# Fixed places for layer 0's maxima units, and bank uses straight behind the values product in 21 of 36 steps

## The reference, cut to what matters

```python
qkv = x @ Wqkv
q = qkv[..., :2 * Hx].reshape(Bx, 2 * NQ, Sx, HD)        # 32 heads of 16
k = qkv[..., 2 * Hx:2 * Hx + G].reshape(Bx, NKV, Sx, HD) # 8 heads, each for 4 query heads
v = qkv[..., 2 * Hx + G:].reshape(Bx, NKV, Sx, HD)
scores = jnp.einsum('bhqd,bhkd->bhqk', q, k) / math.sqrt(HD)
scores = jnp.where(causal, scores, -jnp.inf)
aw = jax.nn.softmax(scores, axis=-1)
aw = aw[:, :, 0] - lam * aw[:, :, 1]
attn = jnp.einsum('bhqk,bhkd->bhqd', aw, v) * (1.0 - LAMBDA_INIT)
```

## Time and profile before

| | us |
|---|---|
| median of 3 runs | 2282.1 |
| lowest, highest | 2281.39, 2282.92 |
| the profiled execution's own time | 2283.89 |
| its span, first to last instruction | 2282.1 |

### The profile page before, as it was taken

How to read it: one execution, slowest core, us unless ns; L and a number is a source line. 1 busy time by engine, 2 the same in 40 slices (tenths; PEclk the granted TensorE clock), 3 DMA queues, 4 the chain that set the end, 5 groups by cost and what they waited for, 6 DMA issues and landing times. The chain is left out here.

```text
span 2282.1 us, 45663 instructions
## 1 busy us (share of the span) xinstructions
PE 2114.3 (93%) x16684; PEld 927.0 (41%) x16684; DVE 1758.6 (77%) x4030; ACT 1551.3 (68%) x3249; POOL 654.6 (29%) x1219
## 2 busy tenths in 40 slices
PE   6799999999999999999999999999999698989983
PEld 5143333333333333333333333333332287567731
DVE  3888888888888888888888888888885277244477
ACT  2078787877878787878787787878787445146633
POOL 2214142332313232414233231313211044000077
PEclk8599999999999999999999999999999799999955
DMA  5230312222121303031222212130200300000001
GB/s 150 41 63 11 67 25 52 38 39 50 27 50 32 65 12 71 10 67 24 54 38 40 50 27 50 32 64 8 45 2 2 103 0 0 1 1 2 1 28 46
DMA packets 129528, 84.74 MB, mean 37 GB/s; under 512 B 90273, under 2 KB 119073, under 8 KB 129313
## 3 DMA queue, kind: packets, MB, share of 16 engines
q1 hardware_dynamic: 129312, 81.91, 18.2%
HBM read 26.81 MB, written 16.78 MB: 19 GB/s over the span
## 5 line engine op out<-in xcount | busy, mean ns | idle before, releaser
L755 ACT ACTIVATE probs<-b_bank 128x512 f32<-128x512 f32 (+1 forms) x2304 | 1171.8, 578 | 347.2 <-PE b_bank L915 336.1
L632 DVE TENSOR_REDUCE m_part<-a_bank 128x1 f32<-128x512 f32 (+3 forms) x2048 | 1190.5, 634 | 153.1 <-PE a_bank L885 111.0
L915 PE MATMUL b_bank<-q_pack,k_pack 34*128 34x512 bf16 (+7 forms) x5120 | 920.8, 348 | 4.4 <-DMA q_pack<-m_rows 2.9
L885 PE MATMUL a_bank<-k_pack,q_pack 64*128 64x512 bf16 (+3 forms) x2560 | 811.1, 357 | 54.3 <-DVE m_part L632 30.7
L957 PE MATMUL acc<-probs,v_tile 128*32 128x512 f32 (+3 forms) x5120 | 586.7, 539 | 3.1 <-POOL probs L498 0.8
L915 PEld LDWEIGHTS b_bank<-q_pack,k_pack 34*128 34x128 bf16 (+1 forms) x5120 | 310.6, 94 | 511.9 <-ACT probs L755 436.3
L885 PEld LDWEIGHTS a_bank<-k_pack,q_pack 64*128 64x128 bf16 x2560 | 226.0, 94 | 343.7 <-DVE m_part L632 209.7
L498 POOL TENSOR_SCALAR_AFFINE_SELECT probs<-probs 128x512 f32<-128x512 f32 (+1 forms) x192 | 151.7, 790 | 609.7 <-ACT probs L755 609.6
L629 DVE CUSTOM_DVE_ANT_0 a_bank<-a_bank,mask_a 128x128 f32<-128x128 f32 (+3 forms) x512 | 241.8, 512 | 66.7 <-PE a_bank L885 66.7
L957 PEld LDWEIGHTS acc<-probs,v_tile 128*32 128x32 f32 x5120 | 107.8, 108 | 174.8 <-issue 117.8
L895 PE MATMUL a_bank<-future,pick 64*128 64x128 bf16 x1024 | 134.4, 219 | 0.0
(11 more groups left out here) (199 smaller groups left out, 1869.9 us busy)
## 6 DMA issues: line engine op xcount, KB each, us to landing
q_pack<-part SPq DMA_DIRECT2D x384, 64.0 KB, 2.3
k_pack<-part SPq DMA_DIRECT2D x192, 64.0 KB, 2.3
headT<-scratch SPq DMA_DIRECT2D x80, 128.0 KB, 4.0
scratch<-qkvT SPq DMA_DIRECT2D x16, 512.0 KB, 2.8
xg<-in_L_attn_x SPq DMA_DIRECT2D x16, 256.0 KB, 2.8
scratch<-qkvT SPq DMA_DIRECT2D x32, 128.0 KB, 2.7
q_pack<-m_rows SPq DMA_DIRECT2D x256, 2.0 KB
x<-in_L_attn_x SPq DMA_DIRECT2D x4, 1024.0 KB, 11.6
```

The source lines that it names most:

```text
L632: dve.tensor_reduce(out, bank[:, 0:w], AX.X, ALU.max).then_inc(a_maxed, 1)
L755: act.activation(probs[:, n % P_RING, h, at:C], b_bank[bank_no(("B", n, h))][:, at:C], ACT.Exp, scale=HD ** -0.5) \
L885: ins = pe.matmul(a_bank[at % A_RING][:, 0:w], q_pack[buf][rows, hp, 0, q:q + P], k_pack[buf][rows, 0, C * c:C * c + w], start=True, stop= ...
L915: ins = pe.matmul(b_bank[bank_no(slot)][:, at:at + C - q], k_pack[par][rows, n2, P * kt:P * (kt + 1)], q_pack[par][rows, h // 2, n2, C * j ...
```

## The change

Five edits, all in layer 0's attention.

- `masked` becomes a fixed set of 12 units instead of the 16 diagonal units of the first pair of heads.
- `schedule()` and its table of times go. `PLACES` gives, for each of the 36 steps, how many units stand in each of five places: woven into heads 0 and 1 (first), behind them and before the values product (between), woven into heads 2 and 3 (second), behind those (behind), and last in the step (last). The sum is still 80 units a group.
- The transposes and projections of a step ("N", "W", "M", "O") stand directly behind the values product, before heads 2 and 3, in the 21 steps of `EARLY`; in the others they stay behind heads 2 and 3. ScalarE takes them in the same order, and the ring of score banks is numbered to match (`SLOTS`).
- "N" moves from step 4 to step 6, the six "W" from steps 6 to 11 to steps 8 to 13.
- VectorE's loop keeps its code; the number of units in a step follows `ENDS`, which now comes from `PLACES`.

```diff
+MASKED = {0, 1, 11, 15, 18, 40, 41, 55, 63, 71, 78, 79}
 def masked(u):
-    j, _, c, hp = A_UNITS[u]
-    return c == j and hp == 0
+    return u in MASKED

-PREP_AT = {4: ("N", 0), **{6 + w: ("W", w) for w in range(WPARTS)}}
+PREP_AT = {6: ("N", 0), 8: ("W", 0), 9: ("W", 1), 10: ("W", 2), 11: ("W", 3), 12: ("W", 4), 13: ("W", 5)}
-ENDS = schedule()
+EARLY = {0, 1, 3, 4, 5, 7, 12, 13, 16, 18, 19, 20, 22, 23, 25, 27, 28, 29, 32, 33, 35}
+PLACES = [[int(units) for units in step] for step in (
+    "11000 01000 01000 10000 11000 11002 11000 11100 11010 11000 11111 11001 "
+    "11000 11000 11000 11100 11000 11000 01000 11001 11000 01110 11000 01100 "
+    "11000 10000 11100 11000 11000 11000 11000 11000 11000 11000 11100 11000").split()]
+ENDS = [sum(map(sum, PLACES[:s + 1])) for s in range(STEPS)]
+def places(n):
+    left = list(units(n)) if n < LAST_STEP else []
+    out = []
+    for count in PLACES[n % STEPS]:
+        out.append(left[:count])
+        left = left[count:]
+    return out

-SLOTS = [slot for n in range(TAIL) for slot in [("B", n, h) for h in range(QH) if n < LAST_STEP] + uses_at(n)]
+SLOTS = [slot for n in range(TAIL) for half in range(2)
+         for slot in [("B", n, 2 * half + h) for h in range(2) if n < LAST_STEP] + uses_at(n) * ((n % STEPS in EARLY) != half)]
...
 # ScalarE
                 for h in range(QH):
                     if n < LAST_STEP:
                         exponential(n, h)
                     if h == 1 and n in COPY_AT:
                         take_output(COPY_AT[n])
+                    if h == 1 and s in EARLY:
+                        take_uses(n)
+                if s not in EARLY:
+                    take_uses(n)
...
 # TensorE
-                if n < LAST_STEP:
-                    two_heads(n, 0, ahead[0] if ahead else None)
+                first, between, second, behind, last = places(n)
+                if n < LAST_STEP:
+                    two_heads(n, 0, first[0] if first else None)
+                for u in between:
+                    score_maxima(u)
                 if LAG <= n < LAST_STEP + LAG:
                     meet_v(n - LAG)
-                if n < LAST_STEP:
-                    two_heads(n, 1, ahead[1] if len(ahead) > 1 else None)
-                for use in uses_at(n):
-                    ...
-                for u in ahead[2:]:
+                if s in EARLY:
+                    turn_and_project(n)
+                if n < LAST_STEP:
+                    two_heads(n, 1, second[0] if second else None)
+                for u in behind:
+                    score_maxima(u)
+                if s not in EARLY:
+                    turn_and_project(n)
+                for u in last:
                     score_maxima(u)
```

More of the change, by code:

```diff
@@ L87 @@
 GATES_AT = 24
[L88 to L109, removed]
-ENDS = schedule()
+EARLY = {0, 1, 3, 4, 5, 7, 12, 13, 16, 18, 19, 20, 22, 23, 25, 27, 28, 29, 32, 33, 35}
[4 more added lines that the diff above has]
+ENDS = [sum(map(sum, PLACES[:s + 1])) for s in range(STEPS)]
 A_LAST = [max(u for u in range(UNITS) if A_UNITS[u][0] == j) for j in range(NJ)]
+LAST_STEP = STEPS * GROUPS
 def units_by(n):
@@ L124, in units @@
     return range(units_by(n - 1), units_by(n))
-LAST_STEP = STEPS * GROUPS
+def places(n):
[5 more added lines that the diff above has]
+    return out
 NEXT = [j for j in range(NJ) if A_LAST[j] < LEAD]
@@ L768, in take_rows_of_output, with take_uses @@
                 act.activation(o_rows[:, :], bank[:, :], ACT.Copy).then_inc(o_taken, 1)
-            for n in range(TAIL):
-                g, s = n // STEPS, n % STEPS
-                for h in range(QH):
-                    if n < LAST_STEP:
-                        exponential(n, h)
-                    if h == 1 and n in COPY_AT:
-                        take_output(COPY_AT[n])
+            def take_uses(n):
                 for use in uses_at(n):
@@ L786, in _ @@
                         take_rows_of_output(k, no, bank)
+            for n in range(TAIL):
+                g, s = n // STEPS, n % STEPS
+                for h in range(QH):
+                    if n < LAST_STEP:
+                        exponential(n, h)
+                    if h == 1 and n in COPY_AT:
+                        take_output(COPY_AT[n])
+                    if h == 1 and s in EARLY:
+                        take_uses(n)
+                if s not in EARLY:
+                    take_uses(n)
                 if g + 2 < GROUPS and s in FIRST_AT:
@@ L969, in _, with turn_and_project @@
                     turn_maxima(m)
[L971 to L978, removed]
-                if n < LAST_STEP:
-                    two_heads(n, 0, ahead[0] if ahead else None)
-                if LAG <= n < LAST_STEP + LAG:
-                    meet_v(n - LAG)
-                if n < LAST_STEP:
-                    two_heads(n, 1, ahead[1] if len(ahead) > 1 else None)
+            def turn_and_project(n):
                 for use in uses_at(n):
@@ L995, in _ @@
                         turn_output(k, bank)
-                for u in ahead[2:]:
+            pe.wait_ge(m_copied, len(NEXT))
+            for n in range(TAIL):
+                g, s = n // STEPS, n % STEPS
+                ahead = list(units(n)) if n < LAST_STEP else []
+                if n < LAST_STEP and s in J_FIRST:
+                    pe.wait_ge(m_rows_in, 16 * QH * (NJ * g + J_FIRST.index(s) + 1))
+                if any(u % UNITS == 0 for u in ahead):
+                    pe.wait_ge(packs_in, 16 * PACK_DMAS * (ahead[-1] // UNITS + 1))
+                first, between, second, behind, last = places(n)
[3 more added lines that the diff above has]
+                    score_maxima(u)
+                if LAG <= n < LAST_STEP + LAG:
+                    meet_v(n - LAG)
+                if s in EARLY:
+                    turn_and_project(n)
+                if n < LAST_STEP:
+                    two_heads(n, 1, second[0] if second else None)
[4 more added lines that the diff above has]
+                for u in last:
                     score_maxima(u)
```

## The result

| | before | after |
|---|---|---|
| median us | 2282.5 (4 runs) | 2458.0 (4 runs, 2456.9 to 2461.9) |
| ratio | 1 | 1.0766, 95% interval 1.0752 to 1.078 |
| span of the profiled execution, us | 2282.1 | 2455.2 |
| one group, product to product, mean us | 106.0 | 117.3 |

The change costs 175 us. The forecast was 2417: the side and the mechanism hold, the size was 41 us short. The measured time lies outside the forecast's own range (2370 to 2450) and 2 us inside the wide one (2320 to 2460).

What follows compares the result with a forecast made beforehand. TensorE's issue order was taken as the bound: 96.0 - 0.4 - 1.0 + 20 of waits = 114.6 us a group against 106.0; over 15.6 groups +134, lead +1, 2282 + 135 = 2417 us. Own range 2370 to 2450, wide 2320 to 2460.

Steps and rivals of the forecast that it cites:

- The deciding term: Second unit's fourth head, before the values product: VectorE frees its bank at 1.18 us, issue wants 0.66, wait 0.52.
- even places win: Rival: the fourth head's wait vanishes and old bunches go; 98.6 us a group, 2167 us; chance 0.08.
- 12 with two units: Gaps between products with a full unmasked first unit and no third: 0.52 us wait each, 6.2 a group.
- 2 with a first unit VectorE masks: Gaps between products where VectorE's masked reduction takes 0.73 us: 0.62 of wait each, 1.2 a group.
- 5 with a narrow or masked first unit: Gaps between products with a narrow or TensorE-masked first unit: 0.2 to 0.4 us wait each, 1.6 a group.
- 10 with three units or more: Gaps between products bound by VectorE, 3.65 us against 2.63 of issue: 1.0 each, 10.5 a group.
- step 2's unit behind `normalise`: Step 2's unit waits 0.5 us for VectorE, which has two masked units, a block maximum and `normalise` first.
- The early uses: Uses directly behind the values product: 7 of 15 a group save a turn, 0 to 1.4 us together, taken as 1.0.
- The rival on ScalarE: In-order ScalarE holds exponentials of heads 2 and 3 behind a use: 7 uses, up to 0.5 us each, 2470; chance 0.04.
- The masks: Four fewer masked units save TensorE 0.44 us a group; VectorE gets 8 more masked reductions, 1.0 us.
- M and O come at least a step after what they read: Early "M" and "O" uses behind the values product were priced at 0 waiting cost.
- The rule on overtaking: TensorE matmuls keep program order, so the 0.52 us counts in full; overtaking by 0.1 would take off 45 us.

Runs made afterwards that it cites:

- experiment 1: The changed kernel with every unit that stood between woven into heads 2 and 3 instead, or put behind; 2347.2 us, ratio 1.0279 to the kernel before.
- experiment 2: The kernel before with each step's second unit issued by itself between heads 0 and 1 and the values product; 2509.5 us, ratio 1.0992.
- 7: The changed kernel with between units woven into heads 2 and 3, and block 2's maxima rows issued ahead of the next group's pack; 2295.6 us, ratio 1.0057.
- 10: The changed kernel with only block 2's maxima rows issued ahead of the next group's pack on SyncE; 2449.5 us, ratio 1.0734 to the kernel before.
- experiment 6: The changed kernel with VectorE's plain reductions over only the first half of a unit's columns; 2338.7 us, ratio 1.0249 to the kernel before.
- 9: The changed kernel with plain reductions halved and block 2's maxima rows issued ahead of the pack; 2279.8 us, ratio 0.9986 to the kernel before.
- experiment 5: The changed kernel with early uses undone, all transposes and projections behind heads 2 and 3 again; 2467.7 us, ratio 1.0809 to the kernel before.
- experiment 3: The kernel before with the early uses alone, in the same 21 steps; 2306.2 us, ratio 1.0099.
- experiment 4: The kernel before with the new set of masked units alone, units per step held at the old list; 2277.2 us, ratio 0.9972.

## Why the prediction was right, and where it was short

**The deciding term held.** The fourth head starts 1.17 us after the first, as forecast from the earlier trace rows, and product to product is 2.93 against a forecast 2.96. Experiments 1 and 2, and the pair 7 and 10, move only the place and move the time both ways; experiment 6, and the pair 9 and 10, move only the length of the reduction and take out 0.27 of that gap. The rival "even places win" was decided by the point it named, and lost.

**The size.** Gap by gap, what is left of each when the issue is taken off at the prediction's prices comes to waits of 22.4 us a group; I had 20. (The same account gives the kernel before 10.7, where I had 10.) These are estimates, since the prices are. The terms as I had set them:

| gaps of a group | forecast | measured |
|---|---|---|
| 12 with two units | 6.2 | 6.8 |
| 2 with a first unit VectorE masks | 1.2 | 1.0 |
| 5 with a narrow or masked first unit | 1.6 | 1.8 |
| 10 with three units or more | 10.5 | 12.3 |
| step 2's unit behind `normalise` | 0.5 | 0.6, and 0.6 in the kernel before too |

The mis-sized term is the ten crowded gaps, which I priced as if all held three units. Those behind steps 5, 10, 11 and 21 hold four or more units, or a unit issued by itself directly ahead of two more: they wait 1.5 to 1.8 each where I had about 1.0. The text let narrow units make up for them, and they do not. Among the twelve, the gap behind step 8 in truth holds a third unit, with a projection between, and waits some 0.8; the one behind step 9 includes some 0.4 for the maxima rows. The step 2 unit was no new wait: its gap is 2.09 us, 2.10 before. The issue itself comes to 94.9 us by this account, where I had 94.6. The two differences, 2.4 and 0.3, are 2.7 us a group, and times 15.6 they are 42 us, where 41 were missing.

**The range** held by luck. It was to cover waits of 14 to 24 us, but by the prediction's own sum 24 gives 118.6 us a group and 2480 us in all, not 2460. The measured time lies 2 us inside the edge; waits of 23 would by the same sum have been outside a range that was meant to hold them.

**The early uses** I put at 1.0 us a group and they gave 0.84 (experiment 5), though I counted seven where there are eight, and one of them costs time: part of the agreement is luck. The bounds 0 to 1.4 were too narrow below: in the kernel before the same edit costs 1.6 (experiment 3). On the four-bank ring a place behind a product can put ScalarE in the way (shown for "N"), and a use may also be cover for VectorE (argued from the steps that lost). The rival on ScalarE had the right engine for "N" in the old step 4, by another path; in the changed list "N" stands in step 6, which is not in `EARLY`.

**The masks** gave 0.34 a group against 0.44 (experiment 4); VectorE's extra work cost at most some tenths.

**SyncE's queue.** I checked the heads' DMAs and not the maxima rows, which stand behind the pack in the same queue. "M and O come at least a step after what they read" looked at the engines and missed what follows an "M". In the changed kernel this costs 8 us in all (experiment 10), hidden by the larger waits; with these gone it is the next bound (experiments 1 and 6).

**The rule on overtaking.** No row of the changed kernel shows the product passing the waiting head: it starts 0.31 behind it (800.40, 800.71). So the 0.52 counts in full. The Trainium skill, "TensorE: Matmul & The Clock Gate", Part 3 (The mechanism), says that matmuls keep their order, and for these two the trace agrees.

**Account of the 175 us.** Between places 154 (experiments 7 and 10); the rows' wait 8 (10); early uses -10 (5); masks -6 (4, measured in the old kernel). The rest, some 29, falls to the new counts per step and the later projections. It is a difference; neither was run by itself.

## What to carry to other kernels

With a ring of n banks between two engines, work out for every pair of neighbours in the issue order how far apart the ring lets them be, and compare it with how far apart the order puts them: moving one item from "woven into" to "right behind" can cost a full wait in every step, while VectorE looks 78% busy (92.0 of 117.3 us here) and TensorE's record says 93% (109.5). Spread such items so that the slow consumer's time passes under work that needs nothing from it, and count gaps with three and four items apart from those with two. A gain in one step is worth only what the next step's engines, and the DMA queue behind them, let through: after each quickened stretch look for the transfer that is now late.

## What the runs showed of the hardware

A stall can cost TensorE twice. In experiment 1 an idle stretch of 2.64 us, at a granted clock of 1.00, was followed by one at 0.71 and one at 0.50, with the same projection at 2.07 us in place of 1.13. It did not follow every time: the clock fell in 10 of the 14 groups that had such a wait. Nor does it take one long stall. Waits of 0.5 us in nearly every step left the clock at 1.00 through the changed kernel's groups until a wait of 1.62 us for the rows near their end (at 1791.6 us, clock at 0.50 from 1799.0). But in experiment 2, whose gaps are longer, it fell to 0.50 in 7 of 16 groups. The 7.30 us before one such fall (668.0 to 675.3) had TensorE on record for 6.36, with no idle stretch over 0.32.

A full-array transpose directly behind a full-array product is nearly free: 1.04 us from product to scores with the short transpose of the maxima, 1.00 without (experiment 3).
